# Feed-forward over routed tokens: rows packed by expert without padding, 32 tiles moved, 39 tile-and-expert items worked from a copy on chip

## The reference

```
x = x + 0.5 * ffn(layernorm(x))        # stage 0 and stage 2
ffn(x): logits = x @ gate_w.T          # 8 experts
        probs = softmax(logits); idx = argmax(probs); w = probs[idx]
        for each expert e: ye = relu(x @ w1[e] + b1[e]) @ w2[e] + b2[e]
        out = ye of the token's own expert * w
```

## Time and profile before

| | |
|---|---|
| median of 3 runs | 1003.09 us (1002.64 to 1005.54) |
| span of the profiled execution | 1001.3 us |
| PE busy | 777.1 us (78%), 5564 instructions |
| DVE busy | 658.6 us (66%), 2367 instructions |
| ACT busy | 507.3 us (51%), 1371 instructions |
| POOL busy | 442.9 us (44%), 563 instructions |
| L832 gathers, both stages | 78, 982 ns each |
| L841 scatters, both stages | 78, 1014 ns each |
| L787 and L799 matmuls, both stages | 624 each, 286 and 287 ns |

### The profile page before, as it was taken

The page is one execution under the profiler, slowest core; times in us unless marked ns, Lnnn a source line. Parts: engine busy times, 40 slices in busy tenths (PEclk is TensorE's granted clock), DMA queues, the critical chain, the costliest instruction groups (busy, mean ns, idle before and its releaser), DMA issues.

```text
span 1001.3 us, 18706 instructions
## 1 busy us (share of the span) xinstructions
PE 777.1 (78%) x5564; PEld 512.1 (51%) x5564; DVE 658.6 (66%) x2367; ACT 507.3 (51%) x1371; POOL 442.9 (44%) x563
## 2 busy tenths in 40 slices
PE   4788983798498960499666979988999899729977
PEld 3678872547288860377651323333333333327757
DVE  4565654775865548856387776877777886566634
ACT  5333331606133323866411466767767677687650
POOL 1047773400277762411156577486585633261100
PEclk9999997895599995699895678999989999959999
DMA  6731113002011113000021342242231200000002
GB/s 154 230 92 49 50 47 99 1 1 84 13 46 52 50 37 82 0 1 1 1 45 32 59 58 37 31 63 34 38 54 31 48 4 3 1 1 1 1 1 84
DMA packets 53426, 42.95 MB, mean 43 GB/s; under 512 B 9861, under 2 KB 48722, under 8 KB 53328
## 3 DMA queue, kind: packets, MB, share of 16 engines
q1 hardware_dynamic: 46784, 31.74, 15.4%
q0 software_dynamic: 4992, 9.32, 3.4%
q10 hardware_dynamic: 1552, 0.70, 0.3%
HBM read 18.27 MB, written 11.40 MB: 30 GB/s over the span
## 4 chain that ended last, share of the span: by engine, by line
PE 42%; DVE 18%; POOL 12%; issue 12%; ACT 9%; DMA 5%; ACTq 1%; DVEq 1%; POOLq 0%; SPq 0%
PE psum L1498 5%; POOL arena L832 4%; DMA result_rows<-arena,scatter_row 3%; PE psum L1269 3%; PE psum L747 3%; DVE half_stats L444 3%; PE psum L1483 2%; DVE cst L1565 2%; PE psum L1232 2%; PE psum L1241 2%; PE psum L1438 2%; PE psum L787 2%; DVE x L694 2%; PE psum L1332 2%; PE psum L799 2%
## 5 line engine op out<-in xcount | busy, mean ns | idle before, releaser
L1565 DVE CUSTOM_DVE_ANT_0 cst<-psum,rot 128x512 bf16<-128x512 f32 (+3 forms) x512 | 219.1, 487 | 64.4 <-PE psum L1470 54.8
L1627 ACT ACTIVATE arena<-psum 128x512 f32<-128x512 f32 (+1 forms) x384 | 178.3, 530 | 51.5 <-PE psum L1483 46.0
L832 POOL DMA_INDIRECT arena<-xhat_rows,gather_row x78 | 76.6, 982 | 148.3 <-DVE gather_row L634 125.2
L1470 PE MATMUL psum<-arena 48*128 48x512 bf16 (+3 forms) x512 | 121.8, 330 | 14.5 <-DVE row_max L1565 10.6
L1483 PE MATMUL psum<-arena 51*128 51x512 bf16 (+3 forms) x512 | 114.9, 315 | 8.8 <-ACT arena L1627 7.1
L1722 POOL TENSOR_SCALAR_AFFINE_SELECT arena<-arena 128x384 f32<-128x384 f32 x128 | 63.6, 521 | 96.4 <-ACT arena L1627 96.4
L1498 PE MATMUL psum<-arena 128*32 128x512 f32 (+3 forms) x1024 | 98.3, 482 | 7.5 <-POOL arena L1725 7.5
L841 POOL DMA_INDIRECT result_rows<-arena,scatter_row x78 | 79.1, 1014 | 30.2 <-issue 22.2
L787 PE MATMUL psum<-arena 128*128 128x128 f32 x624 | 87.5, 286 | 4.2 <-DVE arena L649 4.2
L799 PE MATMUL psum<-arena 128*128 x624 | 89.5, 287 | 0.3
L715 ACT ACTIVATE arena<-psum,gate_b1T 128x128 f32<-128x128 f32 x156 | 48.7, 363 | 68.1 <-PE psum L787 68.1
(11 more groups left out here) (247 smaller groups left out, 1649.1 us busy)
## 6 DMA issues: line engine op xcount, KB each, us to landing
arena<-cut SPq DMA_DIRECT2D x192, 64.0 KB
xhat_rows<-xh SPq DMA_DIRECT2D x16, 256.0 KB, 2.3
arena<-result_rows SPq DMA_DIRECT2D x8, 512.0 KB, 6.0
x<-in_L_attn_x SPq DMA_DIRECT2D x4, 512.0 KB, 7.4
arena<-in_L_ffn_w SPq DMA_DIRECT2D x1, 2048.0 KB, 9.6
out<-x SPq DMA_DIRECT2D x4, 512.0 KB, 3.2
arena<-xhat_rows,gather_row POOLq DMA_INDIRECT x78, 2.5
result_rows<-arena,scatter_row POOLq DMA_INDIRECT x78, 2.3
```

The lines of the kernel that those rows point to most:

```text
L832: pool.indirect_dma_start(xg[:, j % AHEAD, :], None, xhat_dram, bass.IndirectOffsetOnAxis(gather_row[:, j:j + 1], 0)).then_inc(gathered[j ...
L1470: mm = pe.matmul(to[:, col:col + (k + 1) * P], q_stack[b % STACKS][rows, h, k * P:k * P + P], k_stack[b % STACKS][rows, h, 0:(k + 1) * P], ...
L1565: last = nc.vector.tensor_tensor_reduce(masked_scores[:, number % 2, col:col + n_keys], frm[:, col:col + n_keys], mask[:, S - n_keys:], 1. ...
L1627: nc.scalar.activation(prob_e[g % 2][:, j, first:last], bank[MAX_BANKS + number % EXP_BANKS][:, 0:last - first], ACT.Exp, scale=DH ** -0.5 ...
```

## The change

Tokens are packed by expert without padding, so 32 tiles hold them all, and a tile may hold the tokens of several experts. 32 gathers and 32 scatters remain, both by one table `token_of`. What is worked is a list of 39 pairs of a tile and an expert (`ITEMS`): seven breaks between experts cut 32 tiles into at most 39 such pairs. Two tables say the expert and the tile of each item (`expert_of`, `tile_of`). The transposed tiles stay on chip, all 32 (`xgT`, in arena3), so that two items can work on one tile. Each item computes the whole tile with its expert, and `item_mask`, one column for each item, lets through only the lanes of that expert: `result` adds product times mask onto the tile's rows in `y_sorted`, which GpSimd clears first.

Beside this: ScalarE takes three of the four chunks and VectorE one (`BY_DVE = 1`). The numbers are loaded four at a time, `values_load_multi_w_load_instructions`, on TensorE and VectorE from both tables, on ScalarE from one. Eight gathers go ahead instead of six, each with a buffer, and scatters start ten steps late. Scatter of tile t waits for item t + 7. The rank of a token no longer needs an offset for padding, which takes seven small operations and L609 out; five operations for the breaks come in ahead of the wait for the inversion, and four for the mask behind the first two picks. The buffer `mu_t` is moved to arena2.

```diff
-AHEAD = 6
-NOWHERE = 8192
+AHEAD = 8
...
-        xgT = carve(arena4, 2560, (2, P))
+        xgT = arena3[:, 0:T * P]
-        yg = carve(arena4, 4864, (3, D))
+        y_sorted = arena[:, 0:T * D]
...
+            def item_values(engine, table, j, top):
+                last = min(j + 4, ITEMS)
+                return nc.values_load_multi_w_load_instructions(table[0:1, j:last], engines=[engine.engine], min_val=0, max_val=top)[1]
...
-                chain(nc.vector.tensor_scalar(r_ei[:, 0, :], cnt, float(P - 1), None, ALU.add))
...
-                chain(nc.vector.scalar_tensor_tensor(off, r_a, float(P), r_b, ALU.mult, ALU.subtract))
-                chain(nc.vector.tensor_tensor(r_scan[:], r_scan[:], over_t(off), ALU.add))
                 chain(nc.vector.tensor_tensor(flat(r_scan[:]), flat(r_scan[:]), bank[3][:, 0:256], ALU.add))
+                nc.vector.tensor_tensor_scan(cnt_to, one[:, 0:E], cnt, 0.0, ALU.mult, ALU.add)
...
+                chain(nc.vector.tensor_copy(break_int[:, 0, :], starts))
+                chain(nc.vector.tensor_scalar(break_int[:, 1, :], break_int[:, 0, :], 7, None, ALU.logical_shift_right))
+                chain(nc.vector.tensor_copy(break_rank[:, 0, :], break_int[:, 1, :]))
+                chain(nc.vector.scalar_tensor_tensor(break_rank[:, 1, :], break_rank[:, 0, :], float(T - 1), number[:, 1:E], ALU.min, ALU.add))
+                chain(nc.vector.tensor_tensor(item_cmp[:], over_items(break_rank[:, 1, :]), over_breaks(number), ALU.is_le))
                 dve.wait_ge(s["inverted"], at["inverted"] + 1)
...
+                chain(nc.vector.tensor_reduce(expert_f, item_cmp[:], AX.X, ALU.add))
+                chain(nc.vector.tensor_tensor(tile_f, number, expert_f, ALU.subtract))
+                nc.vector.tensor_copy(expert_of[:, 0:ITEMS], expert_f[0:1, :])
+                nc.vector.tensor_copy(tile_of[:, 0:ITEMS], tile_f[0:1, :]).then_inc(s["items_ready"], 1)
...
+                def choose(j):
+                    if j % 4 == 0:
+                        for k, e in enumerate(item_values(dve, expert_of, j, E - 1)):
+                            picked[j + k] = e
+                        for k, t in enumerate(item_values(dve, tile_of, j, T - 1)):
+                            placed[j + k] = t
+                def pick(j):
+                    choose(j)
                     if j >= 2:
                         dve.wait_ge(s["h_mm"], at["h_mm"] + j - 1)
...
-                    nc.vector.tensor_copy(yg[:, k % 3, :], bank[6 + k % 2][:, 0:D]).then_inc(s["y_ready"], 1)
+                    rows = y_sorted[:, bass.ds(placed[j] * D, D)]
+                    nc.vector.scalar_tensor_tensor(rows, bank[6 + j % 2][:, 0:D], item_mask[:, j:j + 1], rows,
+                                                   ALU.mult, ALU.add).then_inc(s["y_ready"], 1)
...
+                chain(nc.vector.tensor_scalar(at_row, tile_f, float(P), cst[:, C_P1:C_P1 + 1], ALU.mult, ALU.add))
+                chain(nc.vector.tensor_tensor(item_cmp[:], over_items(starts), over_breaks(at_row), ALU.is_lt))
+                chain(nc.vector.tensor_reduce(expert_at, item_cmp[:], AX.X, ALU.add))
+                chain(nc.vector.tensor_tensor(item_mask[:], expert_at, expert_f, ALU.is_equal))
...
+                def up(j):
+                    choose(j)
                     pe.wait_ge(s["w1_ready"], at["w1_ready"] + j + 1)
-                    pe.wait_ge(s["xgT"], at["xgT"] + j + 1)
+                    pe.wait_ge(s["xgT"], at["xgT"] + min(j + 1, T))
+                    if j >= 2:
+                        pe.wait_ge(s["hT_ready"], at["hT_ready"] + j - 1)
+                        pe.wait_ge(s["hT_ready_a"], at["hT_ready_a"] + j - 1)
+                    tokens = xgT[:, bass.ds(placed[j] * P, P)]
...
+                if n:
+                    pool.wait_ge(x_done[n], T)
+                pool.memset(y_sorted[:], 0.0).then_inc(s["cleared"], 1)
...
+                def scatter(t):
+                    pool.wait_ge(s["y_ready"], at["y_ready"] + t + E)
...
+                LATER = 10
+                for t in range(AHEAD):
+                    gather(t)
+                for j in range(T + LATER):
+                    if j + AHEAD < T:
+                        gather(j + AHEAD)
+                    if j >= LATER:
+                        scatter(j - LATER)
```

More of the change, by code:

```diff
@@ L657, in hidden, with result @@
                     last.then_inc(s["hT_ready"], 1)
-                def result(j, k, used):
+                def result(j):
                     dve.wait_ge(s["y_mm"], at["y_mm"] + j + 1)
-                    if later(used):
-                        dve.wait_ge(scattered[k % 3], at["scattered"][k % 3] + used)
-                    nc.vector.tensor_copy(yg[:, k % 3, :], bank[6 + k % 2][:, 0:D]).then_inc(s["y_ready"], 1)
-                def six(i):
-                    for k in range(6):
-                        pick(6 * i + k + 2, k + 2)
-                        hidden(6 * i + k + 1, k + 1)
-                        result(6 * i + k, k, 16 * (2 * i + k // 3))
@@ L680, in vector @@
                 chains["f"] = chain.n
-                hidden(0, 0)
-                for i in range(6):
-                    six(i)
-                for j in range(36, ROWS):
-                    if j + 2 < ROWS:
-                        pick(j + 2, j + 2)
-                    if j + 1 < ROWS:
-                        hidden(j + 1, j + 1)
-                    result(j, j, 16 * (j // 3))
+                hidden(0)
+                dve.wait_ge(s["cleared"], at["cleared"] + 1)
+                for j in range(ITEMS):
+                    if j + 2 < ITEMS:
+                        pick(j + 2)
+                    if j + 1 < ITEMS:
+                        hidden(j + 1)
+                    result(j)
                 for g in range(GROUPS):
@@ L764, in tensor @@
                     pe.wait_ge(s["hot_ready"], at["hot_ready"] + t + 1)
-                    last = pe.matmul(bank[2][:, 0:2 * ROWS], lane_hot[:, t, :], tile_hot[:, 0:2, t, :], start=(t == 0), stop=(t == T - 1))
+                    last = pe.matmul(bank[2][:, 0:2 * T], lane_hot[:, t, :], tile_hot[:, 0:2, t, :], start=(t == 0), stop=(t == T - 1))
                 last.then_inc(s["inverted"], 1)
@@ L786, in up, with down @@
                     for c in range(FC):
-                        last = pe.matmul(bank[(2 if c < FC // 2 else 4) + k % 2][:, c * P:c * P + P], w1_tile[:, k % 2, c * P:c * P + P], xgT[:, k % 2, :],
+                        last = pe.matmul(bank[(2 if c < BY_DVE else 4) + j % 2][:, c * P:c * P + P], w1_tile[:, j % 2, c * P:c * P + P], tokens,
                                          start=True, stop=True)
                     last.then_inc(s["h_mm"], 1)
-                def down(j, k):
-                    e = expert(j)
+                def down(j):
+                    e = picked[j]
```

211 lines of the change are left out of this document (100 added, 111 removed).

## The result

The changed kernel takes 1030.29 us (median of 4 runs, 1027.21 to 1031.72); the kernel before, run beside it, 1003.75 us (4 runs). The ratio is 1.0252, with an interval of 1.0218 to 1.0286: it is slower by 2.5%, where 1.2% was forecast, and 1.3 us above the range. The profiled execution has a span of 1025.5 us, 24.2 more than before.

The account below looks back on a forecast made before the run. GpSimd's indirect DMAs bound the kernel before; register loads on TensorE and VectorE would replace them. Stage 0 +4.1, stage 2 +3.4, clock +5, together +12.5 us: 1003.1 + 12 = about 1015 us, range 995 to 1029.

Parts of the forecast that it names:

- GpSimd no longer bounds: Feed-forward loops: 64 indirect DMAs, 82.6 us instead of 100.6, so the bound moves to whatever paces the 39 items.
- The items at 2.01 us, a loop of 76.0: TensorE in the feed-forward loops: 38 periods of 2.01 us with small corrections, 76.0 us without stalls from register loads.
- The lumps decide: Every fourth item, register loads with checks come together, 3.0 us on TensorE and 3.1 on VectorE, and stall the loop.
- The rule weighed against the forecast: TensorE's queue holds 64 instructions, others 8; by depth alone TensorE runs ahead and the loop takes 76.0 us.
- A stall of 2.2 us: Feed-forward loops: the up matmuls of every fourth item start 2.2 us late, nine times a loop, 19.8 us.
- bring it to D+0.8; the lump ends at D+3.8: TensorE's queue: reaches its register loads at D+0.8, finishes them at D+3.8, hands over the up matmuls at D+4.3.
- Late start of the loops: First up matmuls, behind TensorE's first register loads: +3.3 us in stage 0, +2.0 in stage 2.
- The clock: TensorE's clock in the loops: falls to half in three of eighteen stalls, 5 us in all.
- The stages before and after are the same instructions in both kernels, so only the two loops ... count: Outside the two loops over token rows and the ranking ahead of each, nothing changes: no term for later stages.
- the hidden: Rival, feed-forward loops: register loads fit beside work in hand, loop 76.0 us, time 971; chance 0.07.
- half hidden lump: Rival, feed-forward loops: loads of 2.0 us stall 1.1 to 1.2, no clock falls, time 992; chance 0.12.
- The rival of many clock falls: Rival, TensorE in the loops: clock falls after half the stalls or more, +15 us, time 1026; chance 0.20.

Follow-up runs that it names:

- e6: The kernel before with the range check of its one-value register loads left out: 1004.89 us, ratio 1.0009.
- e1: The changed kernel with constants instead of register loads in the loops on VectorE, TensorE and ScalarE: 969.99 us, ratio 0.9662.
- e4: The changed kernel with constants on TensorE and ScalarE, so that VectorE alone keeps its register loads: 1015.25 us, one run.
- e10: e2 with the last group loading items 35 to 38 and TensorE's first group loaded ahead of the first two transposes: 973.14 us, ratio 0.9688.
- e13: As e10, but the last group loads items 36 to 39 from a table padded with a zero: 970.37 us, ratio 0.9658.
- e3: The changed kernel with constants on VectorE and ScalarE, so that TensorE alone keeps its register loads: 1021.76 us, one run.
- e12: The changed kernel once more, unchanged, for a second profile: 1026.43 us, one run.
- e7: The changed kernel with 128 unused bytes a partition ahead of b_in, restoring the addresses of the kernel before: 1028.45 us, ratio 1.0235.
- e9: The changed kernel with expert numbers and tile numbers loaded two items apart on VectorE and TensorE, checks kept: 1009.59 us, ratio 1.0063.
- e11: The kernel before once more, unchanged, for a second profile: 1000.64 us, one run.
- e8: The kernel before with 384 unused bytes a partition ahead of b_in: 1004.22 us, ratio 1.0002.
- e2: The changed kernel with the same four-value register loads but without the range check on each value: 973.06 us, ratio 0.9698.
- e5: The changed kernel with register loads one value at a time, at every item, range check kept: 1020.91 us, ratio 1.0164.

## Why the prediction was right or wrong, point by point

- **GpSimd no longer bounds: right.** It is out of the chain and waits up to 3.6 us in stage 0 and 4.9 in stage 2, and no transpose inside the loops waits for a gather. That it did bound before is read from the chain; e6 fits.
- **The items at 2.01 us, a loop of 76.0: right.** 2.00 or 2.01 between stalls, and 75.9 in e1.
- **The lumps decide: right in mechanism** (e1 to e4), both on TensorE and VectorE, and lengths right: 3.04 and 2.93 us against 3.0 and 3.1. The lump of item 8 starts only at D+1.0, behind the waits of the down group before it (D is defined in the prediction: the end of the down matmuls of item m-3). A queue whose depth counted alone would have given the even 2.0 us of e1. The rule weighed against the forecast was that TensorE's queue holds 64 instructions (the Trainium skill, "TensorE: Matmul & The Clock Gate", header table). No run here shows the depth itself; it did not hide the lumps.
- **A stall of 2.2 us: right in kind, too small, and the first of the two terms that failed.** It is 2.5 on average (2.4 to 2.9), 18 times, some 5.4 us in all. The step was "bring it to D+0.8; the lump ends at D+3.8". From the rows of item 8: D is about 82.9 (L680 starts at 83.11, 0.25 later), the lump starts at 83.9, D+1.0, and ends at D+4.1; L815 starts at 87.34, D+4.4. So TensorE's queue got to the loads 0.2 us later than I had it, and L815 starts 2.4 us later than the 0.11 us behind L797 would have let it. From L815 to L823 it is 0.99 instead of 0.89, which makes the 2.5. In other words, 0.6 us of a lump is hidden, where the forecast's 3.0 and 2.2 hid 0.8. The ninth stall, 2.9, has another cause: its two loads of three values take 0.775 each instead of 0.33, against two range checks fewer (0.6) (e10, e13). I had no term for it; ahead of the run no row showed a load of anything but one value.
- **Late start of the loops: right.** +3.6 and +1.9 against +3.3 and +2.0, and e3 and e4 put it on TensorE's lump. With that lump ahead of the transposes and without the check, e13 has none of it. VectorE's first hidden chunk in stage 2 came 1.5 us later, where 1.8 to 2.1 was forecast.
- **The clock: right in this profile, and by luck in the count**, three falls in 18 stalls and 4.8 us; the forecast took three without working them out. In other executions there are three (e12) or four (e7, the moved copy), at other stalls. Idle times of 2.65 and 2.26 passed without a fall, while 2.41, 2.20 and another 2.26 (at 306.57) had one, so the length of the gap alone does not decide. With stalls of 0.9 (e9) there were none.
- **"The stages before and after are the same instructions in both kernels, so only the two loops ... count": wrong, the second failed term, +6.5 us.** Most of it, 5.4 us, is there when the attention of stage 4 has done 64 of its 512 VectorE operations (L1592): these begin 138.0 us after the last addition of stage 2 before and 138.5 after, the 65th starts at 177.7 and 183.1. The trace shows the wait. The first 20 us of the second batch of transfers `arena<-cut`, kernel before and changed kernel (us, busy by engine, granted clock, DMA share, GB/s):

```profile
546.80:566.80 20.00, 18.66 (x56) 6.96 (x54) 16.27 (x75) 3.74 (x9) 11.70 (x14) 0.50 0.52 81
```

```profile
564.90:584.90 20.00, 18.66 (x56) 6.94 (x54) 16.27 (x75) 3.74 (x9) 11.70 (x14) 0.50 0.56 70
```

The engines do the same work in both, but the transfers move 70 GB/s instead of 81: their packets take 119 ns instead of 94 in the mean, and the 1760 of them start over 23.9 us instead of 19.2. Behind them wait two small transfers `arena<-arena`, and for these TensorE waits (L1483 before is L1510 after):

```profile
566.85 0.60 PE L1483 MATMUL psum<-arena 51*128 51x512 bf16 x1
```

```profile
589.89 0.61 PE L1510 MATMUL psum<-arena 51*128 51x512 bf16 x1 [4.92 <-DMA arena<-arena]
```

Those 4.9 us and the 0.5 above are the 5.4. The wait is absent in the kernel before, in its repetition (e11) and in its moved copy (e8), where the packets take 94 ns each time; in the changed kernel's eleven versions it is 1.2 (e10) to 4.9 us, with packets of 101 to 119 ns. What slows the packets stays open. It is not the 128-byte shift (e7, e8), not the register loads (e1 waits 2.8 us and has 606.9 us in all), and not one odd execution (e11, e12). Nor does it need the packing: e6, the kernel before without its checks, has 98 ns, a wait of 1.0 us and 604.5 us. So what differs seems to come with the built program as a whole; that is argued and not shown. The two terms, 5.4 and 6.5, are the 12 us between forecast and profile.

Of the rivals, the hidden and the half hidden lump fell; the former is what e2 and e13 make of the change. The rival of many clock falls gave a time near the measured one, 1026, for a reason that the profile does not show.

## What to carry to other kernels

A load of a number into a register is work of the queue, and its length counts against what the queue's engine has in hand: here about 0.6 us a visit. Count the instructions of the range check, not the loads; load aligned groups of four without the check where the table is made in range, or, with the check, spread the visits so that each stays near the slack. When a change takes an engine off the path, ask whether the small things it hid fit under the new bound: here they were 3 us lumps, and what could be a gain of 33 us (e13) was a loss of 26.

## What the runs showed that I had not expected

- A TENSOR_LOAD took 0.33 us for four values from a multiple of four, 0.775 for three, and 1.00 to 1.03 for four values from place 35 (TensorE's queue); the very first, in stage 0, took 0.52 to 0.53, but the first in stage 2 0.33.
- Single checked loads and lumps of four cost the loop the same (e5 99.2 and 100.2 us, the changed kernel 100.3 and 101.8), while half lumps cost 7 to 9 us less: 92.7 and 92.8.
- Transfers of stage 4, identical in both kernels, ran slower in every version of the changed one (603.4 to 609.7 us from the last addition on, eleven profiles) than in the kernel before and its moved copy (599.6 to 601.3, three profiles). The kernel before without checks, which has none of the change, lies inside the slower group by its time (604.5).
- The profile named VectorE for TensorE's stops, while TensorE's own lump ended 0.3 us after VectorE's copy of w1. Where several semaphores are waited for, the times on the queue say more than the name.
